# Two adds of the column sums ahead of the second layer's inputs, and a new order of three steps in the last stage

## The chip, the cores and the metric

The kernel runs on one core of a Trainium2 chip. The metric is the device time of one execution, in microseconds (us). The kernel before takes 1113.86 us, the median of 3 runs (1111.87 to 1113.94).

## What is computed

Four parts, each added to x (4096 rows of 128, float32); `adj` is 4096 x 4096, sparse in its values (about one in a thousand off the diagonal is not zero) and stored dense.

```
x = x + gnn_two_layers(layernorm(x), adj, ...)        # per layer: column-normalised, thresholded adj
x = x + moe_ffn(layernorm(x), gate_w, w1, w2, ...)    # top-1 of 8 experts, capacity 640
x = x + adj @ (layernorm(x) * W)
x = x + routed_ffn(layernorm(x), route_id, Wi, Wr, Ws, Wo, ...)

# one layer of the first part
A = M / (sum(M, axis=0) + EPS);  W = where(A > THRESH, A, 0)
T = h @ W_in + b_in
agg = where(has_edge, (W.T @ T) / (sum(W, axis=0) + EPS), T) @ W_out + b_out
out = layernorm(agg + h @ W_self + b_self) * gamma + beta        # then ReLU

# the last part: 64 segments of 64 rows, each with its own expert e of 16, in two layers
h = relu(flat @ Wi.T + bi)
for l in range(2):
    h = relu(h @ Ws[l] + bs[l] + h @ Wr[l, e].T + br[l, e] + h)
out = h @ Wo.T + bo
```

## The kernel before

The kernel is written engine by engine: each engine has its own program, and semaphores tie them together. What an engine's program lists first, it does first; a wait holds up all that is behind it on that engine. All matrix work is float32, so one matmul in the code is two instructions of TensorE in the trace.

`adj` is taken in 8 blocks of 512 columns (`NB` = 8, `BW` = 512). A block is 32 tiles of 128 x 512 (8 MB) and is loaded by SyncE in four quarters of 8 tiles (`load_quarter`) into one of two slots of `ring`. A product of a block is one matmul of 128 x 128 by 128 x 512; 32 of them, summed in PSUM (`products`, line 1457; in the last stage line 1646), make a block. Blocks of the first layer run from the last column block to the first (`blk`).

**First layer.** While TensorE makes the products of block k, VectorE sums the columns of block k+1: a quarter is four adds of 128 x 1024 into `acc` (`add_quarter`, line 892; the first of quarter 0 is not needed), `fold` adds the two halves of `acc` into `pA` (line 900), and TensorE sums `pA` over the partitions (`raw_sums`, lines 1443 and 1445) after 18 products. `verdict` and `mask_if_needed` decide whether the threshold removes anything, `scales` computes the block's factors. TensorE's step also holds small pieces of block k-1 at fixed places between its products (`L1_PIECES`): after 3 and after 8 products the output rows (lines 1473, 1474), after 21 the transposes of the normalised rows (line 1489), after 24 the products with the second layer's weights (line 1500). VectorE's step k is: `collect(k-1)` (line 1037, waits for the last product of the block before), quarter 2 of block k+1, output rows 0 and 1, two adds of quarter 3, output rows 2 and 3, moments, two adds of quarter 3, `fold(k+1)`, quarter 0 of block k+2 around the verdict, mask, scales, `layer2_inputs(k-1)` (lines 1027 and 1028, which copy the results of line 1500 out of PSUM in two halves and add a bias), quarter 1 of block k+2. GpSimd has, for each step, the empty rows (line 755), the moments (lines 767 to 772), `add_bias` (line 761, 128 x 1024) and, once `layer2_inputs` is through, `own_T2` (lines 779 and 781, 128 x 512 each).

**Last stage.** The third part's products of block k (`products3`) alternate with the fourth part's work on block k-1. The places are in `TAIL3`: a number of products, and the piece that follows it. The routed layers of a block are 16 pairs of layer and segment, in four groups of four (`SH` = 4, `NG` = 4): groups 0 and 1 are layer 0, groups 2 and 3 layer 1. For one group:

- VectorE builds a weight for each segment (`stage_w`, line 1335: shared plus routed weight, 128 x 512) in one of four buffers (`WS` = 4). Weight n waits until TensorE has used weight n-4 (`s_wu`).
- TensorE multiplies the group's rows in two pairs (`routed`, line 1689); each pair waits until its two weights are there (`s_wst`). Group 2 also waits for the ReLUs of group 0, and group 3 for those of group 1 (`s_l`).
- VectorE copies the group's result to SBUF (`raw_rows`, line 1345), TensorE transposes it (`turn_routed`, line 1698), and ScalarE applies bias and ReLU to each segment's 64 columns (line 704). For the bias it first reads the segment's route number into a register (`value_load`, line 701). In line 699 it waits for the transposes of the group.

After all four groups TensorE makes the output projection (line 1709) 31 products into the block. The last block's remainder (`last3`) has the same pieces without products between them.

Of the kernel before, what the change touches and what calls it, by code (L numbers as in the profile page):

```python
# [28 lines left out]
ds = bass.ds  # L29
# [9 lines left out]
NB = N // BW  # L39
# [14 lines left out]
E2 = 16  # L54
SEG = N // 64
SB = BW // SEG
KH = DH // P
L2 = 2
SH = SB // 2
NG = L2 * SB // SH  # L60

ORDER2 = (1, 2, 3, 0)
ROWS2 = [t for q in ORDER2[:3] for t in range(q * QT, (q + 1) * QT)] + list(range(BT, QT)) + list(range(BT))
# [15 lines left out]
def build(nc, A, out):  # L79
    ctx = ExitStack()  # L80
    with ctx:
# [113 lines left out]
        route_sb = part(at, N // SEG)[0:1].bitcast(I32)  # L195
# [352 lines left out]
        def _(act):  # L548
# [121 lines left out]
            def step3(k, slot, rnd, prev, nxt):  # L670

                if not prev:

                    for s in range(SB):
                        e = act.value_load(route_sb[0:1, ds((NB - 1) * SB + s, 1)], min_val=0, max_val=E2 - 1)
                        last = nc.scalar.copy(b_last[:, :, s:s + 1], b_r.rearrange("p (lm e) -> p lm e", lm=L2 * KH, e=E2)[:, :, ds(e, 1)])
                    last.then_inc(s_bl, 1)
                    return
                act.wait_ge(s_agg3, k)
                act.wait_ge(s_oTt, k)  # L680
                nc.scalar.activation(oT, PA[1 - slot][:, :], ACT.Copy, scale=w_g[:, 0:1]).then_inc(s_oT, 1)
                act.wait_ge(s_hn3p, k)
                nc.scalar.copy(hT3, T[1][:, :]).then_inc(s_hT3, 1)
                act.wait_ge(s_h0p, k)
                for m in range(KH):
                    last = nc.scalar.activation(h_a[:, m * BW:(m + 1) * BW], O[m][:, :], ACT.Relu, bias=b_i[:, m:m + 1])
                last.then_inc(s_h0, 1)
                if k == NB:
                    for g in range(NG):
                        act.wait_ge(s_la, g + 1)  # L690
                        alone(act)
                        rows = group_rows(g, 0)
                        nc.scalar.activation(rows, rows, ACT.Relu).then_inc(s_l, 1)
                    return
                for n in range(L2 * SB):
                    l, s = n // SB, n % SB
                    dst = (h_b, h_a)[l]
                    if s % SH == 0:
                        act.wait_ge(s_rt, (k - 1) * NG + n // SH + 1)
                        alone(act)  # L700
                    e = act.value_load(route_sb[0:1, ds((k - 1) * SB + s, 1)], min_val=0, max_val=E2 - 1)  # L701
                    for m in range(KH):
                        src = turned(k, n // SH, s % SH // 2, m)[:, s % 2 * SEG:(s % 2 + 1) * SEG]
                        last = nc.scalar.activation(dst[:, m * BW + s * SEG:m * BW + (s + 1) * SEG], src, ACT.Relu,  # L704
                                                    bias=b_r[:, ds(e + (l * KH + m) * E2, 1)])
                    if s % SH == SH - 1:
                        last.then_inc(s_l, 1)
# [142 lines left out]
        def _(dve):  # L850
# [127 lines left out]
            def scales(k):  # L978

                slot = k % 2  # L980
                tb = slice(blk(k) * BT, (blk(k) + 1) * BT)
                nc.vector.reciprocal(rs_, sumc)
                nc.vector.tensor_scalar(nn, ms, 0.0, None, ALU.is_gt)
                nc.vector.tensor_scalar(ne[:, tb], ms, 0.0, None, ALU.is_le)
                dve.drain()
                nc.vector.tensor_tensor(ws_, ms, rs_, ALU.mult)
                dve.drain()
                nc.vector.tensor_scalar(rw_, ws_, EPS, None, ALU.add)
                dve.drain()
                nc.vector.reciprocal(rw_, rw_)  # L990
                dve.drain()
                nc.vector.tensor_tensor(rb[:, tb], rs_, rw_, ALU.mult)
                nc.vector.tensor_tensor(ws_, ws_, rw_, ALU.mult)
                dve.drain()
                nc.vector.tensor_tensor(rbp[slot], rb[:, tb], nn, ALU.mult)
                nc.vector.tensor_tensor(cc[slot], ws_, ne[:, tb], ALU.add)
                dve.drain()
                nc.vector.tensor_tensor(rbp[slot], rbp[slot], ne[:, tb], ALU.add).then_inc(s_msp, 1)
# [40 lines left out]
            def step(k):  # L1039
                if k > 0:  # L1040
                    collect(k - 1)
                if k + 1 < NB:
                    add_quarter(k + 1, 2)
                if k > 0:
                    out_tiles(k - 1, (0, 1))
                if k + 1 < NB:
                    add_quarter(k + 1, 3, (0, 1))
                if k > 0:
                    out_tiles(k - 1, (2, 3))
                    moments(k - 1)  # L1050
                if k + 1 < NB:
                    add_quarter(k + 1, 3, (2, 3))
                    fold(k + 1)
                if k + 2 < NB:
                    add_quarter(k + 2, 0, (0, 1, 2))
                if k + 1 < NB:
                    verdict(k + 1)
                if k + 2 < NB:
                    add_quarter(k + 2, 0, (3,))
                if k + 1 < NB:  # L1060
                    mask_if_needed(k + 1)
                    scales(k + 1)
                if k > 0:
                    layer2_inputs(k - 1)
                if k + 2 < NB:
                    add_quarter(k + 2, 1)

            add_quarter(0, 0)
            add_quarter(0, 1)
# [268 lines left out]
            def raw_rows(k, g):  # L1338
# [3 lines left out]
                if g >= 2:  # L1342
                    dve.wait_ge(s_rt, (k - 1) * NG + g - 1)
                    alone(dve)
# [17 lines left out]
            def step3(k):  # L1362
# [13 lines left out]
                if k < NB:  # L1376
                    for n in range(2, L2 * SB):
                        stage_w(k, n)
                        if n >= 5 and n % SH == 1:
                            raw_rows(k, n // SH - 1)  # L1380
                    raw_rows(k, NG - 1)
                else:
                    for n in range(13, L2 * SB):
                        stage_w(k, n)
                    dve.wait_ge(s_bl, 1)
                    alone(dve)
                    for l in range(L2):
                        for g in (2 * l, 2 * l + 1):
                            raw_rows(k, g)
                        for g in (2 * l, 2 * l + 1):  # L1390
                            relu_rows(k, g)
# [28 lines left out]
        def _(pe):  # L1420
# [280 lines left out]
            def out_proj(k):  # L1701
                if k < NB:
                    pe.wait_ge(s_l, k * NG)
                for t in range(BT):
# [6 lines left out]
                    if t == BT - 1 or k == NB and t == 1:  # L1711
# [1 line left out]


            TAIL3 = [(2, turn_sum), (10, turn_hn3), (12, h0), (14, lambda k: routed(k, 0)), (17, lambda k: routed(k, 1)),
                     (17, lambda k: turn_routed(k, 0)), (19, lambda k: turn_routed(k, 1)), (20, lambda k: routed(k, 2)),
                     (23, lambda k: routed(k, 3)), (23, lambda k: turn_routed(k, 2)), (24, lambda k: turn_routed(k, 3)),
                     (31, out_proj), (NT, None)]

# [90 lines left out]
```

## Time and profile before

| | |
|---|---|
| median of 3 runs | 1113.86 us |
| the profiled execution | 1124.31 us |
| its span on the core | 1122.6 us |
| TensorE busy | 997.6 us, 89% |
| VectorE busy | 578.9 us, 52% |
| ScalarE, GpSimd busy | 323.7 us (29%), 253.6 us (23%) |
| DMA | 220.96 MB, 197 GB/s in the mean |

The first layer takes the span from about 75 to 370 us, the last stage from about 772 us to the end. Of the chain that ended last, 27% of the span are the products of line 1457, 18% those of line 1646 and 11% VectorE's adds of line 892.

In the profile PE is TensorE, PEld its weight loads, DVE VectorE, ACT ScalarE and POOL GpSimd. An arrow in a row points to what released the waiting instruction; "issue" is idle time for which the profile shows no wait. The end of a matmul is modelled, so consecutive rows of PE overlap by some 0.07 to 0.15 us.

### The profile page before, as it was taken

The page shows a single profiled execution, that of the slowest core. Times are in us where ns is not written, and L with a number is a line of the kernel's source. Part 1 is how long each engine was busy: PE and PEld are TensorE (multiplying, and loading weights), DVE is VectorE, ACT ScalarE, POOL GpSimd, SP SyncE. Part 2 cuts the span into 40 slices and gives each one's busy share as a digit, 9 for nine tenths or more (in the row PEclk, how much of TensorE's full clock was granted, in tenths as well). Part 3 has the DMA queues.
Part 4 walks back from the last instruction along what each step waited for, and adds up shares of the span by engine and source line. Part 5 has one row for each costly group of instructions (what it writes and reads, how often), then busy time and mean ns, then how long its engine had stood idle before and what let it go on. Part 6 is the DMA issues. An engine that isn't in the chain of part 4 may idle for free.

```text
span 1122.6 us, 12695 instructions
## 1 busy us (share of the span) xinstructions
PE 997.6 (89%) x3532; PEld 526.3 (47%) x3532; DVE 578.9 (52%) x1553; ACT 323.7 (29%) x646; POOL 253.6 (23%) x246
## 2 busy tenths in 40 slices
PE   0589799999999999999997488838999999999997
PEld 0235445554555544444443266723444544544544
DVE  6877578778732234434333336655235235235365
ACT  3554535654621100000000044315132232232231
POOL 4711213322222112222222113444101101101101
PEclk9889899999999999999999589979999999999999
DMA  9939555555300368888770653214645645645400
GB/s 360 365 151 347 235 191 221 226 225 225 151 1 0 144 265 314 318 309 306 295 313 13 249 187 113 88 38 164 258 185 200 234 166 218 234 158 227 160 1 19
DMA packets 45357, 220.96 MB, mean 197 GB/s; under 512 B 6627, under 2 KB 27941, under 8 KB 33635
## 3 DMA queue, kind: packets, MB, share of 16 engines
q1 hardware_dynamic: 42146, 215.60, 51.2%
q0 software_dynamic: 2864, 4.39, 1.1%
q8 instruction: 28, 0.46, 0.2%
q14 instruction: 47, 0.38, 0.1%
q10 hardware_dynamic: 272, 0.13, 0.0%
HBM read 210.68 MB, written 11.62 MB: 198 GB/s over the span
## 4 chain that ended last, share of the span: by engine, by line
PE 65%; DVE 17%; DMA 4%; issue 4%; DVEq 3%; ACT 2%; ACTq 1%; POOL 1%; another core or an unknown queue 1%; SPq 1%; POOLq 0%
PE PA L1457 27%; PE PA L1646 18%; DVE R L892 11%; PE O L1622 3%; PE O L1689 3%; PE O L1500 2%; DMA ring<-in_adj_cols 1%; DMA work<-disp_d 1%; PE SR L1689 1%; PE SM L1689 1%; PE T L1709 1%; PE O L1668 1%; DVEq L893 1%; ACTq L701 1%; PE T L1698 1%
## 5 line engine op out<-in xcount | busy, mean ns | idle before, releaser
L1646 PE MATMUL PA<-ring,S 128*128 128x512 f32 x512 | 235.2, 599 | 4.4 <-ACT S L667 2.9
L1457 PE MATMUL PA<-ring,S 128*128 128x512 f32 x512 | 235.2, 609 | 3.0 <-POOL S L745 3.0
L1457 PE MATMUL PA<-ring,U 128*128 128x512 f32 x512 | 225.5, 594 | 0.0
L892 DVE TENSOR_TENSOR R<-R,ring 128x1024 f32<-128x1024 f32 x112 | 150.9, 1347 | 8.5 <-issue 2.6
L1457 PEld LDWEIGHTS PA<-ring,S 128*128 128x128 f32 x512 | 98.0, 196 | 108.7 <-issue 104.5
L1457 PEld LDWEIGHTS PA<-ring,U 128*128 128x128 f32 x512 | 95.0, 190 | 107.3 <-issue 107.1
L1646 PEld LDWEIGHTS PA<-ring,S 128*128 128x128 f32 x512 | 92.7, 191 | 104.2 <-issue 99.0
L560 ACT ACTIVATE work<-ring 128x2048 int8<-128x2048 f32 x64 | 122.3, 1910 | 43.6 <-DMA ring<-in_adj_cols 39.5
L1335 DVE TENSOR_TENSOR U<-ring,work 128x512 f32<-128x512 f32 x112 | 81.6, 734 | 85.7 <-PE SR L1689 44.8
L812 POOL DMA_INDIRECT disp_d<-work x32 | 32.3, 1010 | 121.9 <-DVE work L1206 114.6
L844 POOL DMA_DIRECT2D out_x<-work x7 | 5.9, 844 | 235.8 <-DVE work L1406 235.8
L824 POOL DMA_INDIRECT y_d<-R,work x40 | 40.6, 1016 | 70.8 <-DVE R L1266 61.3
L704 ACT ACTIVATE work<-T,work 128x64 f32<-128x64 f32 x112 | 29.2, 310 | 72.2 <-PE T L1698 49.7
L635 ACT COPY work<-T 128x512 f32<-128x512 f32 x8 | 4.7, 585 | 137.7 <-PE T L1545 137.7
L589 ACT ACTIVATE work<-work,small 128x256 f32<-128x256 f32 x32 | 16.6, 589 | 93.3 <-POOL small L772 93.3
L704 ACT ACTIVATE U<-T,work 128x64 f32<-128x64 f32 x112 | 29.0, 310 | 45.7 <-PE T L1698 33.1
L761 POOL TENSOR_TENSOR work<-work,b_all 128x1024 f32<-128x1024 f32 x8 | 18.9, 2360 | 88.5 <-ACT work L581 88.5
L1622 PE MATMUL O<-work,U 128*128 128x128 f32 x320 | 37.3, 276 | 0.8 <-ACT U L649 0.6
L1622 PEld LDWEIGHTS O<-work,U 128*128 128x128 f32 x320 | 36.4, 192 | 1.7 <-ACT U L649 1.7
L1425 PE MATMUL O<-R 128*128 128x256 f32 x4 | 2.1, 674 | 35.7 <-DMA wgate<-in_gate_w 35.7
L1406 DVE TENSOR_TENSOR work<-T,work 128x512 f32<-128x512 f32 x7 | 4.8, 692 | 53.9 <-PE T L1709 53.9
L1689 PE MATMUL O<-U,work 128*64 128x256 f32 x224 | 27.3, 386 | 4.4 <-ACT work L704 4.4
(231 smaller groups left out, 1161.7 us busy)
## 6 DMA issues: line engine op xcount, KB each, us to landing
ring<-in_adj_cols SPq DMA_DIRECT2D x56, 2048.0 KB, 7.7
ring<-in_adjT_cols SPq DMA_DIRECT2D x32, 2048.0 KB, 7.6
ring<-in_Wr SPq DMA_DIRECT2D x1, 4096.0 KB, 12.7
ring<-in_Wr SPq DMA_DIRECT2D x2, 2048.0 KB, 13.3
work<-in_w SPq DMA_DIRECT2D x16, 256.0 KB
disp_d<-U SPq DMA_DIRECT2D x4, 650.0 KB, 12.8
work<-disp_d SPq DMA_DIRECT2D x8, 325.0 KB, 3.1
S<-in_x SPq DMA_DIRECT2D x4, 512.0 KB, 8.9
```

Source lines behind the costliest of these rows:

```text
L560: last = nc.scalar.activation(junk, src, ACT.Gelu, scale=GELU_SCALE, accum_out=csum[slot][:, col:col + 1])
L704: last = nc.scalar.activation(dst[:, m * BW + s * SEG:m * BW + (s + 1) * SEG], src, ACT.Relu, bias=b_r[:, ds(e + (l * KH + m) * E2, 1)])
L761: nc.gpsimd.tensor_tensor(z4, z4, b_all[:, :].unsqueeze(1).to_broadcast([P, BT, DH]), ALU.add).then_inc(s_pre, 1)
L812: nc.gpsimd.indirect_dma_start(disp_d, bass.IndirectOffsetOnAxis(ap=idx[:, t:t + 1], axis=0), rows[:, t * ROW:(t + 1) * ROW], None, bounds ...
L824: nc.gpsimd.indirect_dma_start(y_d, bass.IndirectOffsetOnAxis(ap=e_idx[par][:, q:q + 1], axis=0), e_y[par][:, q * D:(q + 1) * D], None, bo ...
L892: nc.vector.tensor_tensor(acc, ring[slot][0][:, 0:AW] if q == 0 and c == 1 else acc, piece, ALU.add)
L1335: nc.vector.tensor_tensor(dst, ring[0][l][:, ds(e * (KH * DH), KH * DH)], w_s[:, l * KH * DH:(l + 1) * KH * DH], ALU.add).then_inc(s_wst, 1)
L1457: mm = nc.tensor.matmul(out_T[:, :], X[:, t * D:(t + 1) * D], ring[slot][t // HT][:, (t % HT) * BW:(t % HT + 1) * BW], start=n == 0, stop= ...
L1500: mm = nc.tensor.matmul(o, h1T[:, f * BW + t * P:f * BW + (t + 1) * P], W_us[:, f, :], start=f == 0, stop=f == KH - 1)
L1622: mm = nc.tensor.matmul(bank[:, c * D:(c + 1) * D], e_hm[:, f * CAP + q * P:f * CAP + (q + 1) * P], e_w2[par][:, f * D:(f + 1) * D], start ...
L1646: mm = nc.tensor.matmul(PA[slot][:, :], S[:, t * D:(t + 1) * D], ring[1][t // HT][:, (t % HT) * BW:(t % HT + 1) * BW], start=t == 0, stop= ...
L1689: mm = nc.tensor.matmul(LB[g][c * SEG:(c + 1) * SEG, pair * DH:(pair + 1) * DH], src[:, kk * BW + s * SEG:kk * BW + (s + 1) * SEG], weight ...
```

## The change

In the first layer two of the four adds of quarter 1 of block k+2 are put ahead of `layer2_inputs(k-1)`, the other two stay behind it. In the last stage ScalarE reads the route number ahead of the wait for the transposes; VectorE copies the second group after weight 8 where it was after weight 9 (`RAW_AT`; the first and the third group stay after weights 5 and 13); TensorE transposes the second group after 18 products where it was 19, and multiplies the third group (group 2) after 21 where it was 20.

```
+RAW_AT = (5, 8, 13)
...
                 for n in range(L2 * SB):
                     l, s = n // SB, n % SB
                     dst = (h_b, h_a)[l]
+                    e = act.value_load(route_sb[0:1, ds((k - 1) * SB + s, 1)], min_val=0, max_val=E2 - 1)
                     if s % SH == 0:
                         act.wait_ge(s_rt, (k - 1) * NG + n // SH + 1)
                         alone(act)
-                    e = act.value_load(route_sb[0:1, ds((k - 1) * SB + s, 1)], min_val=0, max_val=E2 - 1)
...
                 if k + 1 < NB:
                     mask_if_needed(k + 1)
                     scales(k + 1)
+                if k + 2 < NB:
+                    add_quarter(k + 2, 1, (0, 1))
                 if k > 0:
                     layer2_inputs(k - 1)
                 if k + 2 < NB:
-                    add_quarter(k + 2, 1)
+                    add_quarter(k + 2, 1, (2, 3))
...
                     for n in range(2, L2 * SB):
                         stage_w(k, n)
-                        if n >= 5 and n % SH == 1:
-                            raw_rows(k, n // SH - 1)
+                        if n in RAW_AT:
+                            raw_rows(k, RAW_AT.index(n))
                     raw_rows(k, NG - 1)
...
             TAIL3 = [(2, turn_sum), (10, turn_hn3), (12, h0), (14, lambda k: routed(k, 0)), (17, lambda k: routed(k, 1)),
-                     (17, lambda k: turn_routed(k, 0)), (19, lambda k: turn_routed(k, 1)), (20, lambda k: routed(k, 2)),
+                     (17, lambda k: turn_routed(k, 0)), (18, lambda k: turn_routed(k, 1)), (21, lambda k: routed(k, 2)),
                      (23, lambda k: routed(k, 3)), (23, lambda k: turn_routed(k, 2)), (24, lambda k: turn_routed(k, 3)),
                      (31, out_proj), (NT, None)]
```

## Rows read from the trace of the kernel before

**Rows 1.** The head of the page.
```profile
span 1122.6 us, 12695 instructions
```

**Rows 2.** Waits, 120 to 330 us: who waited for whom, us in total, times, longest.
```profile
DVE U L1027 <- PE O L1500: 18.5, 12, 3.2
...
PE SR L1443 <- DVE work L900: 4.4, 5, 1.1
```

**Rows 3.** Timeline of VectorE, first layer: start, us, engine, line, count [idle before, releaser].
```profile
206.63 0.17 DVE L998 TENSOR_TENSOR small<-small,ne 128x4 f32<-128x4 f32 x1
...
210.15 0.42 DVE L1027 TENSOR_TENSOR U<-O,b_us 128x256 f32<-128x256 f32 x1 [0.97 <-PE O L1500]
210.49 0.41 DVE L1028 TENSOR_TENSOR R<-O,b_us 128x256 f32<-128x256 f32 x1
210.82 6.71 DVE L892 TENSOR_TENSOR R<-R,ring 128x1024 f32<-128x1024 f32 x4
217.82 0.69 DVE L1037 TENSOR_TENSOR work<-PA,U 128x512 f32<-128x512 f32 x1 [0.30 <-issue]
...
334.32 0.69 DVE L1037 TENSOR_TENSOR work<-PA,U 128x512 f32<-128x512 f32 x1 [6.22 <-PE PA L1457]
```

**Rows 4.** Timeline of TensorE, first layer.
```profile
209.83 8.75 PE L1457 MATMUL PA<-ring,S 128*128 128x512 f32 x20
...
237.17 1.13 PE L1443 MATMUL SR<-work,ones 128*128 128x512 f32 x2 [0.74 <-DVE work L900]
...
327.02 8.75 PE L1457 MATMUL PA<-ring,S 128*128 128x512 f32 x20
```

**Rows 5.** Timeline of GpSimd, the same turn.
```profile
207.22 2.37 POOL L761 TENSOR_TENSOR work<-work,b_all 128x1024 f32<-128x1024 f32 x1 [8.69 <-ACT work L581]
211.08 1.85 POOL L779 TENSOR_TENSOR work<-U,ne 128x512 f32<-128x512 f32 x1 [1.50 <-DVE R L1028]
213.08 2.07 POOL L781 TENSOR_TENSOR R<-R,work 128x512 f32<-128x512 f32 x1
```

**Rows 6.** Line 892 by itself: duration in ns, least, median and most; first and last start.
```profile
L892 DVE TENSOR_TENSOR R<-R,ring x112: 1212/1226/2144, 20.4 to 313.3; 128x1024 f32<-128x1024 f32 x112
```

**Rows 7.** Windows of TensorE: stretch, sum, busy (count), granted clock, DMA share, GB/s.
```profile
120.00:125.00 5.00, 4.85 (x14) 0.51 0.07 28
...
155.00:160.00 5.00, 3.88 (x15) 0.90 0.98 365
160.00:165.00 5.00, 5.00 (x18) 0.76 0.14 56
```

**Rows 8.** Waits, 780 to 1100 us.
```profile
PE O L1689 <- ACT work L704: 4.4, 7, 0.8
```

**Rows 9.** Timeline of TensorE, last stage.
```profile
904.21 0.66 PE L1698 MATMUL T<-ident,U 128*128 128x128 f32 x4
...
906.49 1.95 PE L1689 MATMUL O<-U,work 128*64 128x256 f32 x16 [0.76 <-ACT work L704]
...
911.14 1.95 PE L1689 MATMUL O<-U,work 128*64 128x256 f32 x16
...
991.71 1.95 PE L1689 MATMUL O<-U,work 128*64 128x256 f32 x16 [0.47 <-ACT work L704]
```

**Rows 10.** Timeline of VectorE, the same block: weights 8, 12, 14 and 15, and a copy.
```profile
902.00 0.69 DVE L1335 TENSOR_TENSOR U<-ring,work 128x512 f32<-128x512 f32 x1 [1.24 <-PE SM L1689]
...
903.48 0.68 DVE L1345 COPY U<-SM 128x512 f32<-128x512 f32 x1
...
908.42 0.69 DVE L1335 TENSOR_TENSOR U<-ring,work 128x512 f32<-128x512 f32 x1 [3.01 <-PE O L1689]
...
910.50 1.45 DVE L1335 TENSOR_TENSOR U<-ring,work 128x512 f32<-128x512 f32 x2
```

**Rows 11.** The chain that ended last, 899 to 903 us: start, us, what (ACTq is ScalarE's sequencer).
```profile
902.71 0.28 ACTq L701
```

**Rows 12.** Timeline of TensorE's weight loads, the same block.
```profile
912.00 0.63 PEld L1689 LDWEIGHTS O<-U,work 128*64 128x64 f32 x8 [0.24 <-DVE U L1335]
```

More of the change, by code:

```diff
@@ L60 @@
 NG = L2 * SB // SH
+RAW_AT = (5, 8, 13)
 ORDER2 = (1, 2, 3, 0)
@@ L697, in step3 @@
                     dst = (h_b, h_a)[l]
+                    e = act.value_load(route_sb[0:1, ds((k - 1) * SB + s, 1)], min_val=0, max_val=E2 - 1)
                     if s % SH == 0:
@@ L700, in step3 @@
                         alone(act)
-                    e = act.value_load(route_sb[0:1, ds((k - 1) * SB + s, 1)], min_val=0, max_val=E2 - 1)
                     for m in range(KH):
@@ L1062, in step @@
                     scales(k + 1)
+                if k + 2 < NB:
+                    add_quarter(k + 2, 1, (0, 1))
                 if k > 0:
@@ L1065, in step @@
                 if k + 2 < NB:
-                    add_quarter(k + 2, 1)
+                    add_quarter(k + 2, 1, (2, 3))
             add_quarter(0, 0)
@@ L1378, in step3 @@
                         stage_w(k, n)
-                        if n >= 5 and n % SH == 1:
-                            raw_rows(k, n // SH - 1)
+                        if n in RAW_AT:
+                            raw_rows(k, RAW_AT.index(n))
                     raw_rows(k, NG - 1)
@@ L1715, in _ @@
             TAIL3 = [(2, turn_sum), (10, turn_hn3), (12, h0), (14, lambda k: routed(k, 0)), (17, lambda k: routed(k, 1)),
-                     (17, lambda k: turn_routed(k, 0)), (19, lambda k: turn_routed(k, 1)), (20, lambda k: routed(k, 2)),
+                     (17, lambda k: turn_routed(k, 0)), (18, lambda k: turn_routed(k, 1)), (21, lambda k: routed(k, 2)),
                      (23, lambda k: routed(k, 3)), (23, lambda k: turn_routed(k, 2)), (24, lambda k: turn_routed(k, 3)),
```

## The prediction

> **What bounds the kernel now.** I read the waits of each stage before the shares of busy time, because TensorE is busy in nearly every slice and only a wait on the path can be removed. Before it the page gave the span, 1122.6 us [rows 1]; the profiled execution took 1124.31 us, 10.45 us above the median of 1113.86, so I work in differences and set them off from the median. The change touches two stages.
>
> In the first layer VectorE and TensorE hold each other. The waits from 120 to 330 us show TensorE standing 4.4 us in 5 places before the column sums (line 1443), each time for VectorE's `fold` (line 900), and VectorE standing 18.5 us for the second layer's products (line 1500) in 12 places [rows 2]. One turn of this ring is in the two timelines: TensorE gets the folded sums and reaches the products of line 1500; VectorE, idle until then, evacuates the second half of them at 210.15, does a quarter's four adds (6.71 us) and collects at 217.82 [rows 3]; TensorE gets the next folded sums at 237.17 and stood 0.74 us for them [rows 4]. The idle of VectorE behind 206.80 (206.63 plus 0.17) is therefore on the path, though it is idle of an engine that is only half busy over the whole span.
>
> In the last stage TensorE is the bound but for one wait a block: the third group of the routed layers waits for ScalarE's ReLUs of the first group, 4.4 us in 7 blocks [rows 8], 0.76 us in four of them (the row at 906.49 is one) and 0.47 us in three (the row at 991.71) [rows 9].
>
> **First layer: what moves.** In steps 1 to 5 (k > 0 and k + 2 < 8) two of the four adds of quarter 1 go ahead of `layer2_inputs`. Nothing is removed; one wait on a ring semaphore and one tick are added. The quarter has landed by then: in step 1, the tightest, the transfers have fallen to a share of 0.07 in the 120 to 125 us stretch [rows 7], and VectorE comes to the adds behind that.
>
> Step 3 in numbers. Before: free at 206.80, collect at 217.82. After, the two adds start at 206.80. Alone an add takes 1.226 us in the median and 2.144 at most [rows 6], so two take 2.5 us with their gap, and 4.35 at most. They now lie beside GpSimd's `add_bias` (207.22, 2.37 us); before, only evacuations lay beside it. The price of such company is in the same turn: four adds beside the two operations of `own_T2` (211.08 and 213.08, 3.92 us together) [rows 5] took 6.71 us where four alone take 5.1, so 1.6 us for 2 times 512 elements. `add_bias` has 1024, so I take 1.6 us again, nearer to the upper bound: the adds end at 206.80 + 4.1 = 210.9. The Trainium skill, GPSIMD Engine Reference, section "Key points", says that GpSimd shares its SBUF interfaces with VectorE and contends with those VectorE instructions that have two SBUF inputs. By that rule the evacuations, which read PSUM, paid nothing and the moved adds must pay, so it speaks against the change; without it one would put in 2.5 us instead of 4.1, and the sum would stay the same, since the limit below decides. By that rule, the trace agrees: `add_bias`, twice as large, was over in 2.37 us beside evacuations, and the halves took 1.85 and 2.07 us beside adds [rows 5].
>
> Then a drain and a wait (0.3 us, the idle "issue" ahead of 217.82), and both evacuations without idle between them: 2 times 0.75 us (210.15 to 210.49 + 0.41) plus 0.3: done at about 213.0. TensorE does not miss them; it needs those banks again only in the next step, behind 218. Two adds are left beside the first half of `own_T2`: 2.5 + 0.8 = 3.3 us, at most 4.35. They end at 216.3, and VectorE could collect at 216.6.
>
> It can't yet, since the block's products must end first. Where VectorE had nothing else to do, the collect came 334.32 - 327.02 = 7.30 us after the start of the products behind line 1500; in step 3 it came 217.82 - 209.83 = 7.99 us after it [rows 3, 4]. The other four steps concerned show the same 7.99 or 8.00. So the gain is held at 0.69 us a step, with about 0.5 us of VectorE's time to spare. From collect to fold VectorE needs what it needed, so the fold comes 0.69 us earlier against TensorE, whose wait of 0.74 shrinks to 0.05: what is late next is TensorE itself. Five folds (steps 2 to 6): 5 times 0.69 = 3.45 us off the path. Bounds: with 4.35 us for both pairs of adds the collect comes at 206.80 + 4.35 + 0.3 + 1.8 + 4.35 + 0.3 = 217.9, so nothing is gained; the best case is the 3.45. `own_T2` starts some 2 us later; the next work in GpSimd's queue is not due before 220, so that costs nothing while it ends by then. ScalarE's queue and SP's refills are not moved.
>
> **Last stage: three edits.** (a) ScalarE's route number is read ahead of the wait on the turned rows. The chain shows 0.28 us of register work of line 701 between TensorE's end and the first ReLU, with its bounds checks about 0.5 us [rows 11]. So group 0's ReLUs are done about 0.5 us earlier, at about 905.95 instead of 906.45. (b) VectorE copies group 1 after staging weight 8, not 9. (c) TensorE turns group 1 one product earlier and begins group 2 one product later (0.86 us: 20 instructions, two a product, take 8.75 us with the modelled end of the last [rows 4]).
>
> Edit (c) makes (a) of no use, and this is where I chose. Without its wait group 2 would have started at 906.49 - 0.76 = 905.73; one product later is 906.59, behind ScalarE's 905.95. The wait is gone, but group 2 starts 0.10 us later than before, and in the three blocks with 0.47 us 0.39 later. VectorE stages the weights of group 3 in four buffers, each set free only by group 2's own products: weight 12 starts 1.93 us after group 2 (908.42), weights 14 and 15 end at 910.50 + 1.45 = 911.95 [rows 10], 5.46 us after it. The second pair of group 3 waits for them; before, it got its first weight load at 912.00 with VectorE as the releaser, just in time [rows 9, 12]. After, group 3 starts without a wait at 911.14 - 0.76 = 910.38, wants its second pair 0.94 us later (half of the row's 1.95 less its modelled end), at 911.32, and gets it at 911.95 + 0.10 + 0.05 = 912.10. So the wait for ScalarE is replaced by 0.78 us for VectorE inside group 3. The second pair began at 911.14 + 0.94 = 912.08: a loss of 0.02 in four blocks, and of 0.39 - 0.08 = 0.31 in three. Sum: 4 x 0.02 + 3 x 0.31 = 1.0 us slower.
>
> Edit (b) is needed by (c). The turn of group 1 is now due at 904.21 - 0.86 = 903.35; weight 8 ends at 902.69 and the copy (0.68 us) then ends at 903.37 at the latest, against 904.16 before [rows 9, 10]. That is no wait, and no slack. Weights 9 to 11 are queued behind the copy and end where they ended, over 1 us ahead of group 2. Bounds of the stage: all 4.4 us of idle recovered, or each turn late by one staging more (0.69 us and 0.18 of issue, 0.87 us): 7 x 0.87 + 1.0 = 7.1 us lost. I take 1.0 us, the value by the order of events, as both ends need a row to be elsewhere than it is.
>
> **Sum.** -3.45 + 1.0 = -2.45 us: 1122.6 becomes about 1120.15, and 1113.86 becomes 1111.4, or 0.22% less. About 0.2% (2.2 us) is what a measurement of this kernel can tell from no change.
>
> **Rivals.**
> 1. *The adds' company eats the gain.* `add_bias` and `own_T2` slow both pairs of adds to 2.14 us each; the collect stays at 217.9. For it: the maximum of 2.144 [rows 6]. Against: only the middle two of four adds can have paid much in 6.71 us. Then 0 + 1.0: 1114.9. Chance 0.15.
> 2. *A clock dip goes too.* In step 2 the granted clock was 0.90 and 0.76 in two stretches of 5 us around and behind the fold wait [rows 7], so partly at 1.2 instead of 2.4 GHz, worth (0.10 + 0.24) x 5 = 1.7 us; with 0.69 us less of idle it may stay at 1.00. Then 1113.86 - 4.15 = 1109.7. Against: it had been at 0.51 in the stretch from 120 to 125 us already, and the cause may lie there, which isn't touched. Chance 0.17.
> 3. *The idle of the last stage is really recovered*, because VectorE's staging of 12 to 15 starts sooner than I say. Then -3.45 - 4.4: 1106.0. Against: the row at 912.00 names VectorE as the releaser. Chance 0.08.
> 4. *Slower: the turn of group 1 comes too early.* Place: line 1698 for group 1, waiting for the copy of line 1345; a late copy delays group 2, hence the staging, hence group 3. Price: one staging, 0.87 us as above, in 7 blocks: 6.1 us, -2.45 + 6.1 = +3.65, 1117.5. It makes the kernel measurably slower from a wait of (2.2 + 2.45) / 7 = 0.66 us. For it: no slack in 903.35 against 903.37. Against: the products that the copy waits for end before the turn of group 0, and ScalarE has that one by 902.71 [rows 11]. Chance 0.08.
> 5. *The change does nothing*, as a staging or ReLU that I have off the path is on it: 1113.9, chance 0.04.
>
> **How the numbers follow.** The forecast itself has 0.48, and its own range is 1109.9 to 1113.4 (the layer's gain 1.5 to 3.45 us, the last stage 0.5 better to 1.0 worse). The range for all is 1107.0 to 1115.4: it leaves out rival 3, rival 4 and little else. Faster by over 0.2%: 0.28 of the forecast's 0.48, rivals 2 and 3, together 0.53. Slower: rival 4 and a little beyond it, 0.09. Within 0.2%: the rest, 0.38.
>
> **What the profile after would show.** Right: in steps 2 to 5 VectorE's collect waits for TensorE and comes 7.3 us after the start of the products, and the wait of line 1443 for line 900 falls from 4.4 to about 1 us (of steps 2 and 6, where it was 1.1). Adds at 1.9 us or more ahead of the evacuations. In the last stage the wait of line 1689 for line 704 is gone, a wait of line 1689 for line 1335 of 0.5 to 0.8 us in 7 blocks stands in its place, and the block's period stays within 0.05 us of 42.75 in the first blocks and grows by about 0.3 in the last three. Wrong: a period of about 42.0 (rival 3) or 43.5 (rival 4), a collect later than 7.8 us after the products' start (rival 1), or a clock below 1.00 in a stretch where it was 1.00 before.

## The result and the profile after

| | before | after |
|---|---|---|
| median, first comparison | 1113.27 us (4 runs) | 1106.49 us (1104.69 to 1106.89, 4 runs) |
| median, second comparison | 1111.31 us (18 runs) | 1105.70 us (1104.78 to 1106.47, 7 runs) |
| the profiled execution, its span | 1124.31, 1122.6 us | 1106.10, 1104.3 us |

The ratio is 0.9939 (95% interval 0.9923 to 0.9954) in the first comparison and 0.9952 (0.9934 to 0.9969) in the second: faster by 5.6 to 6.8 us, where 2.45 us were forecast. The forecast range, 1107.0 to 1115.4, missed the first median by 0.5 us. The two spans differ by 18.3 us, of which 12.3 belong to one execution and not to the change: in the profiled execution of before an expert took 11.7 us instead of the 9.66 us of every other profile here.

The page of after, head:

```profile
span 1104.3 us, 12701 instructions
## 1 busy us (share of the span) xinstructions
PE 993.8 (90%) x3532; PEld 527.4 (48%) x3532; DVE 587.6 (53%) x1553; ACT 328.0 (30%) x646; POOL 250.1 (23%) x246
```

**First layer.** VectorE's timeline of the turn that [rows 3] shows of before. VectorE's and GpSimd's lines are shifted by one (892 is now 893, 1027 is 1028, 1037 is 1038), TensorE's by three (1443 is 1446, 1457 is 1460, 1500 is 1503).

```profile
204.38 4.53 DVE L893 TENSOR_TENSOR R<-R,ring 128x1024 f32<-128x1024 f32 x2
209.14 0.42 DVE L1028 TENSOR_TENSOR U<-O,b_us 128x256 f32<-128x256 f32 x1 [0.23 <-issue]
...
210.14 0.41 DVE L1029 TENSOR_TENSOR R<-O,b_us 128x256 f32<-128x256 f32 x1
210.47 3.19 DVE L893 TENSOR_TENSOR R<-R,ring 128x1024 f32<-128x1024 f32 x2
214.74 0.69 DVE L1038 TENSOR_TENSOR work<-PA,U 128x512 f32<-128x512 f32 x1 [1.07 <-PE PA L1460]
```

TensorE and GpSimd in the same turn:

```profile
207.45 8.75 PE L1460 MATMUL PA<-ring,S 128*128 128x512 f32 x20
...
234.10 1.12 PE L1446 MATMUL SR<-work,ones 128*128 128x512 f32 x2 [0.28 <-DVE work L901]
```
```profile
204.83 2.99 POOL L762 TENSOR_TENSOR work<-work,b_all 128x1024 f32<-128x1024 f32 x1 [8.69 <-ACT work L582]
```

The collect now waits 1.07 us for TensorE and comes 214.74 - 207.45 = 7.29 us after the start of the products, where it came 7.99 us after [rows 3, 4]. TensorE's wait for the fold, 0.74 us there [rows 4], is 0.28. The waits from 120 to 330 us, against the 18.5 and 4.4 us of [rows 2]:

```profile
DVE work L1038 <- PE PA L1460: 13.0, 6, 6.2
...
DVE U L1028 <- PE O L1503: 3.2, 2, 2.3
...
PE SR L1446 <- DVE work L901: 1.8, 5, 0.6
```

**Last stage.** Timelines of TensorE, its weight loads and VectorE, for the block that [rows 9, 10, 12] show of before. Lines 1689, 1698, 1335 and 1345 are now 1692, 1701, 1338 and 1348.

```profile
884.05 0.66 PE L1701 MATMUL T<-ident,U 128*128 128x128 f32 x4
...
887.22 1.95 PE L1692 MATMUL O<-U,work 128*64 128x256 f32 x16
...
891.01 1.08 PE L1692 MATMUL O<-U,work 128*64 128x256 f32 x8
892.74 0.44 PE L1692 MATMUL O<-U,work 128*64 128x256 f32 x2 [0.65 <-DVE U L1338]
```
```profile
892.74 0.20 PEld L1692 LDWEIGHTS O<-U,work 128*64 128x64 f32 x4 [1.10 <-DVE U L1338]
```
```profile
883.31 0.68 DVE L1348 COPY U<-SM 128x512 f32<-128x512 f32 x1
...
889.15 0.69 DVE L1338 TENSOR_TENSOR U<-ring,work 128x512 f32<-128x512 f32 x1 [2.99 <-PE O L1692]
...
891.23 1.46 DVE L1338 TENSOR_TENSOR U<-ring,work 128x512 f32<-128x512 f32 x2
```

And the waits of the stage, 770 to 1090 us, against the one of [rows 8]:

```profile
PE O L1692 <- DVE U L1338: 4.5, 7, 0.7
```

Group 2 starts without a wait (887.22), and the second pair of group 3 stands until the weights that end at 891.23 + 1.46 = 892.69 are there. 4.4 us of waiting for ScalarE have become 4.5 us of waiting for VectorE. The copy of group 1 ends at 883.99, the turn starts at 884.05.

To compare kernels, two sums from TensorE's rows of each profile are used below: **the layer's five steps**, from the start of line 1500's products in step 1 to those in step 6 (before 126.04 to 323.57, 197.53 us; after 127.09 to 318.81, 191.72 us), and **the stage's six periods**, from group 0 of one block to group 0 six blocks on (before 809.96 to 1065.94, 255.98 us; after 790.62 to 1047.36, 256.74 us; these starts are those of the chain that ended last). Beside them stands the mean granted clock of all runs of a kernel, since by the estimate worked out below it carries about half of the gain. Each ratio is to the runs of before taken beside that kernel. Where a field is empty, the sum was not taken.

| kernel | median us (runs) | ratio, interval | mean clock | five steps | six periods |
|---|---|---|---|---|---|
| before, beside the first four | 1111.31 (18) | | 0.9646 | 197.5 in both profiles | 256.0 |
| after | 1105.70 (7) | 0.9952 (0.9934 to 0.9969) | 0.9671 | 191.7 | 256.7 |
| adds only | 1103.56 (6) | 0.9931 (0.9912 to 0.9951) | 0.9677 | 191.7 | |
| last stage only | 1112.69 (12) | 1.0011 (0.9997 to 1.0026) | 0.9644 | 195.8 | 256.8 |
| new places only | 1112.20 (10) | 1.0010 (0.9998 to 1.0022) | 0.9644 | 197.5 | 256.8 |
| number only | 1107.64 (11) | 0.9969 (0.9952 to 0.9985) | 0.9639 | 195.8 | 252.6 |
| adds and number | 1100.92 (6) | 0.9910 (0.9888 to 0.9932) | 0.9665 | 191.8 | |
| adds, late fold | 1112.85 (12) | 1.0009 (0.9983 to 1.0036) | 0.9639 | 201.1 | |
| four adds ahead | 1106.17 (4) | 0.9948 (0.9929 to 0.9967) | 0.9667 | 193.2 | |
| adds, number on both engines | 1102.32 (6) | 0.9921 (0.9906 to 0.9937) | 0.9650 | 191.7 | 252.5 |
| whole change, number on both engines | 1099.66 (4) | 0.9897 (0.9869 to 0.9925) | 0.9670 | 191.8 | 252.4 |

### The profile page after: what moved, and what is told of

Read it like the earlier page. It is cut to its first block, busy times and chain, and to the rows that moved or that the text cites. A ratio compares the mean times of both kernels' runs of the same rounds, so it can differ in the third digit from the quotient of the medians.

```text
span 1104.3 us, 12701 instructions
## 1 busy us (share of the span) xinstructions
PE 993.8 (90%) x3532; PEld 527.4 (48%) x3532; DVE 587.6 (53%) x1553; ACT 328.0 (30%) x646; POOL 250.1 (23%) x246
## 4 chain that ended last, share of the span: by engine, by line
PE 70%; DVE 14%; issue 4%; DVEq 3%; DMA 3%; ACT 3%; POOL 1%; SPq 1%; ACTq 0%; POOLq 0%
PE PA L1460 31%; PE PA L1649 18%; DVE R L893 8%; PE O L1625 3%; ACT U L650 3%; PE O L1503 3%; PE O L1692 2%; DMA ring<-in_adj_cols 2%; PE T L1701 1%; PE SR L1692 1%; PE SM L1692 1%; PE T L1712 1%; PE O L1671 1%; DVEq L894 1%; PE SR L1446 1%
## 5 line engine op out<-in xcount | busy, mean ns | idle before, releaser
L893 DVE TENSOR_TENSOR R<-R,ring 128x1024 f32<-128x1024 f32 x112 | 156.5, 1397 | 8.9 <-issue 3.2
L1338 DVE TENSOR_TENSOR U<-ring,work 128x512 f32<-128x512 f32 x112 | 83.9, 754 | 84.3 <-PE SR L1692 43.6
L762 POOL TENSOR_TENSOR work<-work,b_all 128x1024 f32<-128x1024 f32 x8 | 21.5, 2688 | 88.0 <-ACT work L582 88.0
## 6 DMA issues: line engine op xcount, KB each, us to landing
work<-in_w SPq DMA_DIRECT2D x16, 256.0 KB
```

The costliest lines, as they stand in the source:

```text
L893: nc.vector.tensor_tensor(acc, ring[slot][0][:, 0:AW] if q == 0 and c == 1 else acc, piece, ALU.add)
L1338: nc.vector.tensor_tensor(dst, ring[0][l][:, ds(e * (KH * DH), KH * DH)], w_s[:, l * KH * DH:(l + 1) * KH * DH], ALU.add).then_inc(s_wst, 1)
```

## The experiments

Theory: the layer gives the whole gain, the last stage loses a little. Rivals: the last stage gains too, or the two profiles differ for another reason than the change.

**Before, once more**, for a second profile.

> The kernel before, unchanged, for a second profile. In the two profiles so far the stage of the experts differs by 12.3 us, though no line of it was changed: 11.7 us an expert in the profile of before, where VectorE waits 13.5 us for rows of y to be stored, and 9.66 us in the profile of after. Theory A: this is how that one execution of before went, and an ordinary one has 9.66 us an expert; then this profile is near 1112 us, with no such wait, and the first layer's steps 3 to 5 still take 38.9 to 39.3 us. Rival B: the slow experts belong to the kernel before, and the change cures them by another route (times of the loads); then this profile is near 1124 us with 11.7 us an expert.

Measured: 1112.13 us, every expert 9.66 us. Theory A holds; the slow experts were of one execution. Its five steps took 197.52 us, as much as in the first profile, but the loss stands elsewhere. In the first, the clock was low behind the fold of step 2 [rows 7]; here it is low behind that of step 6. Windows of TensorE, then its timeline there:

```profile
310.00:315.00 5.00, 3.88 (x9) 1.00 0.00 0
315.00:320.00 5.00, 5.00 (x15) 0.66 0.00 0
```
```profile
314.50 1.12 PE L1443 MATMUL SR<-work,ones 128*128 128x512 f32 x2 [1.11 <-DVE work L900]
316.27 4.52 PE L1457 MATMUL PA<-ring,S 128*128 128x512 f32 x6
```

The same place in the kernel with only the last stage changed, whose first layer is that of before:

```profile
312.80 1.13 PE L1445 MATMUL SR<-work,ones 128*128 128x512 f32 x2 [1.11 <-DVE work L902]
314.57 2.82 PE L1459 MATMUL PA<-ring,S 128*128 128x512 f32 x6
```

Same code, same wait of 1.11 us: in one execution TensorE drops to 1.2 GHz for a while behind it, and six instructions take 4.52 instead of 2.82 us. A dip costs 1.70 us, and whether it comes is not fixed by the program.

**Only the adds ahead.**

```
+                if k + 2 < NB:
+                    add_quarter(k + 2, 1, (0, 1))
                 if k > 0:
                     layer2_inputs(k - 1)
                 if k + 2 < NB:
-                    add_quarter(k + 2, 1)
+                    add_quarter(k + 2, 1, (2, 3))
```

> Only the two adds go ahead of the second layer's inputs; the last stage is as before. Theory A: all of the gain is here: the five first-layer steps together 5.6 us shorter (3.9 us of waits, 1.7 us of a clock dip), ratio 0.9940 to 0.9955, about 0.7 us faster than the whole change. Rival B: the last stage carries a part of the measured gain that the two profiles hide; then the ratio stays above 0.9965.

Measured: 0.9931, 1103.56 us: all of the gain, and more. The expected ratio was 0.9940 to 0.9955, so the gain was forecast too low here as well.

**Only the last stage changed.**

```
+                    e = act.value_load(...)
                     if s % SH == 0:
                         act.wait_ge(s_rt, (k - 1) * NG + n // SH + 1)
                         alone(act)
-                    e = act.value_load(...)
...
-                        if n >= 5 and n % SH == 1:
-                            raw_rows(k, n // SH - 1)
+                        if n in RAW_AT:
+                            raw_rows(k, RAW_AT.index(n))
...
-                     (17, lambda k: turn_routed(k, 0)), (19, lambda k: turn_routed(k, 1)), (20, lambda k: routed(k, 2)),
+                     (17, lambda k: turn_routed(k, 0)), (18, lambda k: turn_routed(k, 1)), (21, lambda k: routed(k, 2)),
```

> Only the last stage is changed (number ahead of the wait, second copy and third group moved), the first layer is as before. Theory A: the wait of line 1689 for ScalarE (4.4 us) is replaced by one for VectorE's weights (4.5 us); the stage's period is 42.8 us; ratio 1.0000 to 1.0015. Rival B: below 0.9985, the stage gains when it isn't behind the other change. The clock dip of step 2 in the first layer should be there if it belongs to the wait before the fold.

Measured: 1.0011, six periods of 256.77 us against 255.98. No gain; in the times no change that can be told, in the periods a loss of 0.8 us (and from the seventh group 0 to the end of the span after took 56.94 us where before took 56.66).

**The whole change again.**

> The whole change, unchanged, beside the other two on one chip. Theory A: 0.9939 within its interval (0.9923 to 0.9954), a little slower than the adds alone; experts at 9.66 us each in the profile; no clock dip in step 2. Rival: the 0.9939 was partly luck of the runs, and the ratio is 0.9955 to 0.9965, what the two stages' profiles add up to (5.6 - 0.8 = 4.8 us).

Measured: 0.9952, 1105.70 us; no dip behind a fold in its profile. The median lies 2.1 us above the adds alone, where the stage's loss is 1.1 and the clock's 0.0006 x 1106 = 0.7; the 0.3 us left are small against the intervals.

Next, the question which part of the last stage does what, and whether the dips hang on the wait before the fold.

**Only the number ahead of ScalarE's wait** (the first part of the diff above).

> Only the route number is read ahead of ScalarE's wait; the order of the groups and the first layer are as before. Theory A (the third group's new place and the staging of its successor's weights eat what the number gives): alone the number lets group 2 start 0.54 us earlier in four blocks and 0.47 in three, and the weights 12 to 15 with it, so the stage's period falls from 42.75 to about 42.2 us, the wait of line 1689 for ScalarE from 4.4 to about 0.8 us, no wait for VectorE appears: 3.6 us, ratio 0.9965 to 0.997. Rival B: the weights hold group 3 in any case; then the period stays at 42.7 and the ratio at 1.000.

Measured: 0.9969, 3.4 us faster, periods of 42.2 and 41.95 us. One of its blocks, TensorE:

```profile
886.87 1.95 PE L1689 MATMUL O<-U,work 128*64 128x256 f32 x16 [0.23 <-ACT work L704]
...
891.52 1.95 PE L1689 MATMUL O<-U,work 128*64 128x256 f32 x16
```

The wait is 0.23 us where it was 0.76 [rows 9], and group 3 runs without one. The rival, that the weights hold group 3 in any case, falls.

**Only the new places** (the other two parts of that diff).

> Only the new places: second copy after weight 8, turn of group 1 after 18 products, group 2 after 21. ScalarE reads the number behind its wait as before, and the first layer is as before. Theory A (the new place of group 2 makes ScalarE's earlier end worthless, since the weights for group 3 decide): the same last stage as with the number ahead, period 42.8 us, a wait of about 0.65 us for VectorE in 7 blocks and none or under 0.1 us for ScalarE; ratio 1.000 to 1.0025, as last_only. Rival B: ScalarE's later ReLUs now hold group 2 or 3 by some tenths; period 43.1 us or more, ratio above 1.003.

Measured: 1.0010, six periods of 256.77 us, 4.5 us of waits for VectorE in 7 blocks: to a few hundredths the stage of the whole change. With the new places the number ahead is worth nothing, as the prediction's choice had it.

**Adds and number, old places.**

> The two adds ahead and the number ahead, without the new places of copy and groups. Theory A: 1.0 us of the last stage's loss is gone and 3.6 us gained: 3.6 us below the adds alone (1103.6), about 1100.0, 4.6 to 5.7 us below the whole change; last-stage period 42.2 us. Rival B: within 1 us of the adds alone.

Measured: 0.9910, 1100.92 us, 2.6 us below the adds alone and 4.8 below the whole change. Theory A predicted 3.6 and 4.6 to 5.7. Its clock was 0.9665 against 0.9677 of the adds alone, worth 1.3 us; the rest fits.

**The whole change, and the number ahead of VectorE's wait too.**

```
+                e = dve.value_load(route_sb[0:1, ds((k - 1) * SB + s, 1)], min_val=0, max_val=E2 - 1)
                 if k < NB:
                     dve.wait_ge(s_wu, (k - 1) * (L2 * SB) + n + 1)
                     alone(dve)
                 dst = wst[n % WS] if k < NB else last_w[n]
-                e = dve.value_load(route_sb[0:1, ds((k - 1) * SB + s, 1)], min_val=0, max_val=E2 - 1)
```

> The whole change, and VectorE too reads the route number ahead of its wait (line 1334 ahead of 1331), so that weights 12 to 15 start about 0.5 us sooner behind group 2. Theory A: the new wait in group 3 (0.65 us) falls to about 0.15 us, the last stage's period from 42.8 to about 42.3 us, the time by about 3.5 us against the whole change, to about 1102. Rival C: the wait in group 3 stems from VectorE's work itself, not from what it does between wait and first add; then the wait stays above 0.5 us and the time at 1105.5.

Measured: 0.9897, 1099.66 us, the fastest here, 6.0 us below the change. TensorE, then VectorE, in one block:

```profile
884.52 1.95 PE L1693 MATMUL O<-U,work 128*64 128x256 f32 x16
...
888.31 2.20 PE L1693 MATMUL O<-U,work 128*64 128x256 f32 x16
```
```profile
885.85 0.69 DVE L1339 TENSOR_TENSOR U<-ring,work 128x512 f32<-128x512 f32 x1 [2.25 <-PE O L1693]
```

Weight 12 starts 1.33 us after group 2 (884.52 to 885.85) where it took 1.93, group 3 is through in 2.20 us as one piece, and the period is 42.07 us. No row of TensorE names a wait there, but the 2.20 us are 0.25 more than the 1.95 of a group without one, and the weight loads name VectorE inside it (889.42, 0.48 us): about 0.25 us of the 0.65 are left, where theory A had 0.15. The time between wait and first add was the price, not VectorE's work: rival C falls. Theory A had a period of 42.3 us and 1102 us, a smaller gain than measured.

**The same with the old places.**

> Adds ahead and the number ahead of the wait on both engines, without the new places of copy and groups. Theory A (the new places only shift a product from one side of group 2 to the other; what counts is that neither ScalarE nor the weights are late): period between 42.1 and 42.3 us as in adds_and_number, with the wait of 0.23 us for ScalarE still there in some blocks, 1100 to 1101. Rival B: the new places are worth something once the weights come sooner: then all_and_vector_number (1099.7) is faster by 1 us or more.

Measured: 0.9921, six periods of 252.54 us against 252.41, with the wait for ScalarE still there in three blocks (0.35 us). The medians differ by 2.7 us, but so do the clocks (0.9650 and 0.9670, 2.2 us), and the intervals overlap. So the stage's periods give the new places 0.1 us; whether they are worth more is not decided.

**Adds ahead, and the fold made late again.** In steps 1 to 6:

```
                     add_quarter(k + 1, 3, (2, 3))
+                    if k > 0:
+                        nc.vector.tensor_tensor(acc[:, 0:BW], acc[:, 0:BW], acc[:, 0:BW], ALU.max)
+                        dve.drain()
                     fold(k + 1)
```

> The adds alone, and in steps 1 to 6 of the first layer one more operation on VectorE (a maximum of the sums with themselves, 0.69 us and its gap, which changes nothing) right ahead of the fold. So the order of the adds is the new one, but TensorE waits for the fold as long as before (0.7 to 1.4 us). Theory A (a longer wait there is what lets the granted clock fall in some executions): the five steps are back at about 195.5 to 196 us without a dip; the mean clock of the runs falls from 0.967-0.969 to 0.963-0.966, the runs spread over 3 us or more, and the median is 5.5 to 8 us above the adds alone. Rival B (the clock's dips have to do with where the adds stand, not with the wait): the clock stays at 0.967-0.969 and the median is 3.8 to 4.2 us above the adds alone, with a spread under 2 us.

Measured: 1112.85 us, 9.3 us above the adds alone, more than the 5.5 to 8 that theory A gave; 12 runs from 1106.39 to 1119.73 us, with clocks from 0.971 to 0.957. Six of its windows:

```profile
155.00:160.00 5.00, 3.60 (x14) 0.89 0.98 367
160.00:165.00 5.00, 5.00 (x17) 0.77 0.12 52
275.00:280.00 5.00, 3.52 (x13) 0.84 0.88 374
280.00:285.00 5.00, 5.00 (x18) 0.82 0.00 0
315.00:320.00 5.00, 3.95 (x16) 0.94 0.00 0
320.00:325.00 5.00, 5.00 (x17) 0.72 0.00 0
```

Three dips, each behind a fold wait (1.40, 1.48 and 1.05 us; two more waits of 1.04 and 1.15 us went without). The five steps took 201.07 us, which is 3 x 1.70 = 5.1 more than 195.97. The adds stand where the change puts them, the wait is back, and so are the clock's losses: rival B, that the place of the adds matters to the clock by itself, falls. The waits are longer than those of before (1.04 to 1.48 against 0.73 to 1.12 us), so the size of the loss is that of this kernel and not of before.

**All four adds ahead**, the rest as in the whole change.

> The whole change, but all four adds of the quarter ahead of the second layer's inputs. Theory A (since the change the products' end holds the collect, and VectorE has about 1.1 us to spare): the collect still comes 7.3 us after the start of the products behind line 1500, the five steps stay at 191.9 us within 0.5, the time within 2 us of the whole change. Rival B: GpSimd's two operations on the second layer's rows now start so late (by 3 us) that they lie beside collect and quarter 2 and slow these; then the steps grow by 0.5 to 1 us each and the wait before the fold is back at 1 us, with the clock's dips.

Measured: 0.9948, 1106.17 us, but 193.23 us for the five steps and waits of 0.56 to 0.93 us before the fold. Neither theory is whole: the collect still waits for TensorE (1.58 us), so the products' end still holds it, and yet in four of the five steps 0.3 to 0.6 us are lost behind it. In step 4 VectorE and GpSimd show where:

```profile
213.65 6.33 DVE L894 TENSOR_TENSOR R<-R,ring 128x1024 f32<-128x1024 f32 x4
```
```profile
212.81 1.27 POOL L783 TENSOR_TENSOR R<-R,work 128x512 f32<-128x512 f32 x1
216.04 1.55 POOL L757 TENSOR_TENSOR U<-U,work 128x512 f32<-128x512 f32 x1 [1.96 <-ACT work L576]
```

Quarter 2 lies beside both GpSimd operations and takes 6.33 us instead of about 6.04. In step 3 it takes 6.04 as with the adds alone, and what is lost there is a pause of VectorE that the next section shows. The idle in front of the collect is no free place for GpSimd's work to slide past.

## Why the prediction was wrong

**The layer's mechanism held.** The collect was forecast at 7.30 us behind the start of the products and came at 7.29; its limit is the products' end. The adds under `add_bias` were costed at 4.1 us (at most 4.35) and took 4.53. Line 893 by itself, 204.3 to 209.5 us, durations in ns:

```profile
L893 DVE TENSOR_TENSOR R<-R,ring x2: 1226/2225/3224, 204.4 to 205.7; 128x1024 f32<-128x1024 f32 x2
```

The first took 1.23 us and the second 3.22, far more than the maximum of [rows 6]: it ends at 208.9, 1.1 us behind GpSimd's operation (204.83 + 2.99 = 207.82). So the bound of 4.35 was none. That used up some of the slack and changed nothing: the drain and the evacuations behind them took 1.64 us (208.91 to 210.55) instead of 1.8, the other two adds 3.2 instead of 3.3, and of the 1.07 us of idle ahead of the collect about 0.8 was to spare, where 0.5 was expected (0.3 is the drain and wait that [rows 3] has too).

**The term of the layer was too small.** 3.45 us were forecast; without a dip the five steps went from 195.82 (last stage only, number only) to 191.71 us (adds only), 4.1 us. From step to step, up to steps 2, 3, 4, 5 and 6, the gains are 0.68, 1.05, 0.69, 0.69 and 1.00 us. So 0.69 a step was right, and in steps 3 and 6 some 0.3 us came on top. There the sentence failed that "from collect to fold VectorE needs what it needed": from the collect to the fold it took 18.97 and 18.96 us in these two steps (last stage only) and 18.62 and 18.67 (adds only), against 18.60 in steps 4 and 5 of both. In before VectorE pauses in them, in step 3 ahead of the output rows and in step 6 inside quarter 3; the first two rows are those of before, the third is that of after in the place of the first:

```profile
185.81 0.42 DVE L1009 TENSOR_TENSOR work<-O,work 128x256 f32<-128x256 f32 x1 [0.67 <-issue]
...
306.38 1.23 DVE L892 TENSOR_TENSOR R<-R,ring 128x1024 f32<-128x1024 f32 x1 [0.45 <-issue]
```
```profile
183.42 0.42 DVE L1010 TENSOR_TENSOR work<-O,work 128x256 f32<-128x256 f32 x1 [0.30 <-issue]
```

In steps 4 and 5 the idle ahead of these instructions is 0.30 us and none. The profile names no releaser for the pauses. They stand in the same two steps in all kernels with the first layer of before, and with four adds ahead they are back (18.98 and 19.26 us, the second with slowed adds as well). In step 2 the 18.98 us stayed the same. What the pauses wait for is open.

The other part of the forecast that was off is where TensorE loses the time. Its wait for the fold kept 0.28 us a step instead of 0.05. The rest of the 0.69 stood in a place that was not looked at: the second pair of output rows (line 1473), which waits for VectorE's line 1011. TensorE's timeline of before, then of after, from the products ahead of those rows to the products behind them:

```profile
221.44 4.46 PE L1457 MATMUL PA<-ring,S 128*128 128x512 f32 x10
225.88 0.67 PE L1473 MATMUL O<-W_io,work 128*128 128x256 f32 x2
...
227.68 8.75 PE L1457 MATMUL PA<-ring,S 128*128 128x512 f32 x20
```
```profile
219.06 4.45 PE L1460 MATMUL PA<-ring,S 128*128 128x512 f32 x10
225.07 8.75 PE L1460 MATMUL PA<-ring,S 128*128 128x512 f32 x20
```

The same work took 227.68 - 221.44 = 6.24 us before and 6.01 after. In steps 1 and 7 of before, where VectorE is not pressed, it takes 6.02. So a wait of 0.23 us stood there in each of the five steps, covered by the modelled end of the matmul before it, so that no row calls it idle; only the 0.67 us of the pair of line 1473, otherwise 0.59, hints at it. Seen from TensorE the 4.1 us are 5 x 0.23 = 1.1 us of this wait and 3.0 us of the waits that the rows name (4.4 and 0.36 before, 1.8 after).

**The last stage held, step by step.** Group 2's wait went, group 3's second pair waits for the weights, the copy of group 1 comes just in time (883.99, turn at 884.05), the periods are 42.79 us throughout, so 0.04 us more in the first blocks and 0.31 in the last. Forecast 1.0 us slower, measured 0.76 in six periods and 0.28 behind them. Only the wait is 0.65 us by its row instead of 0.78. The first median, 1106.49, lies near the 1106.0 of rival 3, but by chance: its sign, a period of about 42.0 us, did not come.

**The step that failed is the second rival, the clock's term, put at nothing in the sum.** The clock dip was taken as one event of 1.7 us in one execution, with a chance of 0.17 to go, and was kept out of the forecast. Its size was right (1.70). But the dip is not an event of step 2. In the first layer it comes behind fold waits of about 1.1 us, and only in some executions: in step 2 in one profile of before, in step 6 in the next and in that of the new places, in none of two other kernels with the same first layer. The forecast was to be the median of many executions, and for that a chance of dips in all of them had to be counted. In the seven profiles with the adds ahead and nothing added, whose waits there are 0.2 to 0.9 us, none follows.

What the clock carries can be estimated from its mean. At half the clock TensorE takes double the time, so where TensorE sets the pace a mean that is lower by d costs about d times the span. The runs of one kernel bear this out: over the 22 runs of before that stand beside the number alone, a clock listed lower by 0.001 goes with 1.0 us more. From 0.9646 to 0.9671 it is 0.0025 x 1106 = 2.8 us. The layer's 4.1 us less the 1.1 that the last stage loses are 3.0, which makes 5.8 us; measured were 5.6 in the second comparison and 6.8 in the first. Compared at the same clock, the four runs of before listed at 0.966 have a mean of 1109.7 us and the three of after 1106.4, 3.3 us less, near those 3.0. For the adds alone: 0.0031 x 1106 + 4.1 = 7.5, measured 7.75. For the number alone: 3.4 us in six periods and 0.5 in the seventh block, less 0.0006 x 1108 = 0.7 for a clock that was lower (0.9639 against 0.9645 of the 22 runs of before beside it): 3.2, measured 1111.08 - 1107.64 = 3.4. For the late fold against the adds alone: 0.0038 x 1110 = 4.2 and 195.97 - 191.71 = 4.3 us of added waits: 8.5, measured 9.3. The account closes to within 1 us each time. It rests on clocks listed to three decimals.

So the forecast of 2.45 us less was near the part that is in the program (3.0), and lacked the part that is in the clock. The median of 1113.86 us from which the range was set off also lay 2.5 us above the 1111.31 us of the 18 runs later.

**What is open.** The late fold shows that a longer wait before the fold lowers the mean clock; it does not show that all of the 0.0025 comes from there. Only one execution of each kernel has a profile. In the five with the first layer of before there are three dips behind the fold, 3 x 1.70 / 5 = 1.0 us an execution, less than the 2.8 us by the clocks; three of these five executions were faster than most of their kernel (listed at 0.966, 0.968 and 0.969, where the means are 0.9639 to 0.9644). Kernels with the adds ahead differ among themselves, from 0.9677 (adds only) down to 0.9650 (adds, number on both engines), though their fold waits are alike. And dips of the same 1.7 us stand elsewhere. Where the last stage begins, TensorE waits 2.86 us for ScalarE in every kernel, and in 5 of the 13 profiles, of kernels with and without the adds ahead, the clock is low behind it. In that of before, TensorE's timeline and windows:

```profile
772.79 7.54 PE L1646 MATMUL PA<-ring,S 128*128 128x512 f32 x13 [2.86 <-ACT S L667]
```
```profile
770.00:775.00 5.00, 2.21 (x4) 0.84 0.85 315
775.00:780.00 5.00, 5.00 (x11) 0.82 0.25 105
```

The time up to step 1 varies too, from execution to execution and not with the change: the turn of line 1481 in step 1 begins at 91.3 to 93.2 us in kernels with the same code up to there, at 92.2 and 93.2 in the profiles of before and at 93.2 and 92.1 in those of after.

## What to carry to other kernels

A wait of 1 us on TensorE cost here its length and the chance that the clock falls behind it; for a forecast of a median, both go into the sum, and two or three profiles of the same kernel tell a chance from an event. When a wait is about to be removed by moving work behind it, look for who had been sized to that wait: here the weights of the next group, whose staging kept pace only with the old order, and the better edit was to shorten what lies between a wait and the first useful instruction, on both engines (1099.66 us against 1105.70). Filling VectorE's idle time in front of a wait cost nothing here while GpSimd's work, released later, did not slide into the stretch behind it.

## What the runs showed of the hardware

- An add of 128 x 1024 on VectorE takes 1.23 us alone; one that began 0.9 us behind the start of GpSimd's 128 x 1024 operation took 3.22 us and ended 1.1 us behind that operation's end. GpSimd's operation took 2.99 us beside adds against 2.37 beside evacuations from PSUM. The slowing is mutual, and dearer than the 1.6 us that were worked out from [rows 5]: the two adds paid 2.0 us. The Trainium skill, GPSIMD Engine Reference, section "Key points", names such VectorE instructions, with two SBUF inputs, as the ones that contend; these rows agree.
- After a wait of 1.04 to 1.48 us before the fold TensorE's granted clock fell in 6 of 15 cases (3 of 10 in five profiles with the first layer of before, 3 of 5 in the late fold); after the shorter waits before the fold in none. After the wait of 2.86 us ahead of the last stage it fell in 5 of 13. In each of these places a dip is worth 1.7 us by the windows.
- Between a satisfied wait and the first instruction, reading a number into a register cost 0.5 us on ScalarE (group 2 comes 5.91 us behind group 1 instead of 6.43) and 0.6 us on VectorE (1.33 instead of 1.93 us from group 2 to weight 12).
